# All PSUM banks as one ring in program order, the first layer's weighting in column halves, and a new order of a group's steps

## Chip, cores and metric

One core of one Trainium2 chip. The metric is the device time of one execution in microseconds (us).

## The reference

Four cross-attention layers run one after another on x (64 batches x 64 tokens x 256 features), each against the same context ctx (64 x 64 x 256). Inputs are float32, the mask is all ones in the drawn inputs, and the weights of all layers are inputs too.

```
L0 (channels = the 64 tokens): Mn = Wn inorm(x) + bn;  Mm = Wm inorm(ctx) + bm;  A = softmax(Mn' Mm) over 256
                               x = Wo (Ml A') + bo + x,  Ml = Wl ctx + bl
L1, L2 (16 heads of 16):       a = layer_norm(ctx) * gamma + beta;  Q = x Wq', K = a Wk', V = a Wv'
                               x = x + tanh(gate) * (softmax(mask(Q K' / 4)) V) Wo'
L3 (one head):                 q = x w_q', k = ctx w_k', v = ctx w_v'
                               x = x + alpha * (softmax(q k' / 16) v) w_o'
```

## The kernel before

The 64 batches are cut into 8 groups of 8 (`GB`), four pairs of batches (`NP`) of 128 tokens each. A prologue prepares the weights and the first group's "front" (transposes of x and ctx, their normalised forms, Mn, Mm, V0). Then a loop runs seven times over one group, with the front of the next group worked in, and an eighth, last group follows without a front.

What stands in a group is a list of steps made by `group_order` (from line 37 on). Every engine walks the same list and does its own part of each step. A step (kind, layer, i) is one of:

- P name i, a projection or transpose by TensorE into one PSUM bank: K, V, Q (keys, values, queries of a layer), AT (transposed attention output), O (output projection), XN, PV (last layer's output), and in the front xT, cT, nT, Mn, Mm, V0. An E step of the same name says where ScalarE and VectorE take the result out of the bank, where that isn't the place of the P step itself.
- S l i, scores. Layers 0 to 2 have eight, which TensorE makes in pairs (i even makes i and i + 1, each in 64 rows of the array, line 565 or 582). VectorE takes the maximum (lines 916, 920) and, in layers 1 and 2, subtracts it (line 924), which releases the bank. In layer 0 the exp on ScalarE reads the bank and releases it.
- X l i, the exp on ScalarE (lines 749, 755).
- T l i, transposes of the exps by TensorE (lines 608, 615), copied from PSUM by ScalarE (line 767). In layers 1 and 2 a T step fills two banks.
- A l i, the weighting of the values by TensorE (line 635 in layer 0, line 652 in layers 1 and 2), then division by the sums on VectorE. In layer 0 two A steps share a bank; in layers 1 and 2 the two batches of a pair go to partitions 0 to 63 and 64 to 127, in 64-column halves of the array.
- ST, MV, SC: statistics and moments of the next group's rows, and the sum columns, on VectorE.

Projections of layers 1 to 3 are made of a high and a low part of each operand, three products (lines 361 to 363). The low part of attnT is `o - hi` on VectorE (line 888), of the state it is line 857, and O waits for the first, Q for the second. Queries go from PSUM to `qe` in two copies on ScalarE (line 732), value rows in four (line 719), keys in one (line 712), whose rows GpSimd spreads into `kbd` (line 1119).

The eight PSUM banks are four rings of two: `proj`, `scores`, `turned`, `weighted`. The dictionary `RING` puts xT, cT, nT and V0 into the `weighted` ring. Before a fill TensorE waits until the fill two before in the same ring is released; `*_full` and `*_free` semaphores of each bank count fills and releases. In the prologue all eight banks serve as one ring.

The layer 0 weighting, from line 633:

```
for u in range(2):
    for s in range(2):
        mm_ = pe.matmul(o[:, (2 * (i % 2) + u) * V0W:(2 * (i % 2) + u + 1) * V0W],
                        probsT[:, i % 4, D * s + P * u:D * s + P * u + P], v0[:, i, s, :], start=s == 0, stop=s == 1)
```

SyncE loads the next group (`load_group`, lines 318 to 321) once the proj banks' fills of the group before are counted and `normed` and `mix_ready` are reached, and stores the result in two parts (line 334). It waits for the landed store at the end of a pass, so the next pass's load is issued behind it. GpSimd makes `mix`, the reciprocal deviations and the normalised rows (`front`, lines 1140 to 1161), between spreading the keys of layer 1 and of layer 2. The first scores of layer 2 wait for that second spreading.

Of the kernel before, what the change touches and what calls it, by code (L numbers as in the profile page):

```python
# [17 lines left out]
ALU = mybir.AluOpType  # L18
# [18 lines left out]
def group_order(front):  # L37
# [17 lines left out]
    def S(l, i):  # L55
        return at("S", l, i)
# [64 lines left out]
RING = {"xT": "A", "cT": "A", "nT": "A", "V0": "A"}  # L121


def build(nc, x, ctx_in, mask, w, cst, out):
# [8 lines left out]
    def numbered(order, kind):  # L133
        n, at = 0, {}
        for s in order:
            if kind == "A" and s[0] == "A" and s[1] == 0:
                at[s] = n
                n += s[2] % 2
            elif (RING.get(s[1], "P") if s[0] == "P" else s[0]) == kind:
                per = 2 if kind == "T" and s[1] in (1, 2) else 1  # L140
                at[s] = n
                n += per
        return at, n

    p_at, p_n = numbered(ORDER, "P")
    p_at_last, _ = numbered(LAST_ORDER, "P")
    pro_steps = [s for s in PROLOGUE if s[0] == "P"]
    p_at_pro, p_n_pro = {s: n for n, s in enumerate(pro_steps)}, len(pro_steps)
    s_at, s_n = numbered(ORDER, "S")
    t_at, t_n = numbered(ORDER, "T")  # L150
    a_at, a_n = numbered(ORDER, "A")
    assert p_n % 2 == 0 and s_n % 2 == 0 and t_n % 2 == 0 and a_n % 2 == 0

    pro_bank = {s: (n + 2 - p_n_pro) % 8 for s, n in p_at_pro.items()}
    PRO_FILLS = [list(pro_bank.values()).count(i) for i in range(8)]
    P_BASE = PRO_FILLS[0]
    assert P_BASE == PRO_FILLS[1] > 1

    def p_count(g, step, last):

        if g is None:
            bank_of = pro_bank[step]
            return bank_of, sum(pro_bank[s] == bank_of and n <= p_at_pro[step] for s, n in p_at_pro.items())
        n = (p_at_last if last else p_at)[step]
        return n % 2, g * (p_n // 2) + (P_BASE + n // 2 + 1)

    def ring_count(g, n, total):


        fills = g * (total // 2) + (n // 2 + 1)  # L170
        return n % 2, fills, g * (total // 2) + (n // 2 + 2)

    with ExitStack() as stack:
# [75 lines left out]
        negmax = sb("negmax", [P, 2, NJ])  # L249
        shifted = sb("shifted", [P, 2, 512])  # L250
# [16 lines left out]
        bl_wide, bo_row = result[:, 0, 0:P], result[:, 1, 0:C]  # L267

        scores = [bank("scores0"), bank("scores1")]
        turned = [bank("turned0"), bank("turned1")]  # L270
        weighted = [bank("weighted0"), bank("weighted1")]
        proj = [bank("proj0"), bank("proj1")] + scores + turned + weighted

# [37 lines left out]
        def _(sp):  # L311
# [11 lines left out]
            def iteration(g, last):  # L323
                if not last:

                    for i in range(2):
                        hold(proj_full[i], g * (p_n // 2) + P_BASE)
# [909 lines left out]
```

## Time and profile before

| | us |
|---|---|
| median of 3 runs | 837.75 (830.71 to 838.94) |
| profiled execution: its time | 832.73 |
| profiled execution: its span, first to last instruction | 830.9 |
| mean granted TensorE clock of that execution | 0.978 |
| matmuls | 7362 |

The profile is of one execution. A row's time is from the start of its instruction to its end; the ends of matmuls are modelled, so that the distance from one step's first row to the next step's is a better measure of a step than its busy time. PE is TensorE's matmuls and PEld its weight loads. A fp32 matmul stands as two instructions, each with its load. "idle before <-X" means that the engine stood before the instruction and X let it go.

### The profile page before, as it was taken

The numbers are of one execution on the slowest core, as the hardware profiler recorded it, in microseconds if no ns is written. First come the engines' busy times: TensorE is split into PE (matmuls) and PEld (weight loads), VectorE is DVE, ScalarE is ACT, GpSimd is POOL, SyncE is SP. The second block draws the span as 40 slices with busy tenths as digits, with TensorE's granted clock in tenths as the row PEclk, the third lists the DMA queues.
The fourth block names the chain that finished last, engine by engine and source line by source line (L and its number), as shares of the span: only waits on it lengthen the run. The fifth ranks groups of instructions, "written<-read, shape, count | busy, mean of one in ns | idle before, by whom it ended". The sixth has DMA issues, their size and how long they took to land.

```text
span 830.9 us, 19359 instructions
## 1 busy us (share of the span) xinstructions
PE 719.0 (87%) x7362; PEld 645.1 (78%) x7362; DVE 526.5 (63%) x1148; ACT 459.1 (55%) x909; POOL 199.8 (24%) x169
## 2 busy tenths in 40 slices
PE   2689889988998889998899889998899888988886
PEld 2578788877888788887788778887888877878775
DVE  4957567675676656674675746756566745745565
ACT  1486555655547555565556555475554655546452
POOL 3543400442004700136004420047001360010000
PEclk9899999999999999999999999999999999999999
DMA  7010000200001000200002000010002000000000
GB/s 207 27 55 1 2 2 0 79 0 0 0 26 53 0 0 0 79 0 0 0 0 79 0 0 0 25 54 0 0 0 79 0 0 0 0 27 2 1 2 26
DMA packets 18805, 17.14 MB, mean 21 GB/s; under 512 B 2206, under 2 KB 18718, under 8 KB 18782
## 3 DMA queue, kind: packets, MB, share of 16 engines
q1 hardware_dynamic: 16854, 15.38, 5.7%
q10 hardware_dynamic: 1608, 1.18, 0.5%
q0 software_dynamic: 320, 0.27, 0.2%
q8 instruction: 15, 0.25, 0.1%
q14 instruction: 8, 0.07, 0.0%
HBM read 12.63 MB, written 4.19 MB: 20 GB/s over the span
## 4 chain that ended last, share of the span: by engine, by line
PE 52%; DVE 22%; ACT 14%; issue 10%; DMA 1%; DVEq 1%; ACTq 0%; POOL 0%
PE proj L361 8%; PE scores L582 8%; DVE negmax L920 8%; PE proj L362 7%; PE proj L363 7%; DVE shifted L924 5%; ACT work L732 4%; PE weighted L635 3%; PE scores L565 3%; PE turned L615 3%; ACT v L719 3%; PE turned L608 3%; DVE attnT_lo L888 2%; PE weighted L652 2%; ACT work L749 2%
## 5 line engine op out<-in xcount | busy, mean ns | idle before, releaser
L767 ACT ACTIVATE work<-turned 128x512 f32<-128x512 f32 (+1 forms) x208 | 114.0, 580 | 106.2 <-PE turned L615 70.7
L1119 POOL TENSOR_TENSOR kbd<-k_tmp,own_row 128x1024 f32<-128x1024 f32 x32 | 60.3, 1894 | 444.5 <-ACT k_tmp L712 444.5
L755 ACT ACTIVATE work<-shifted 128x512 f32<-128x512 f32 x128 | 80.6, 631 | 86.4 <-DVE shifted L924 86.3
L920 DVE TENSOR_REDUCE negmax<-scores 128x8 f32<-128x512 f32 x128 | 87.4, 683 | 45.2 <-PE scores L582 45.2
L582 PE MATMUL scores<-kbd,work 64*128 64x128 f32 x1024 | 75.3, 286 | 42.0 <-DVE shifted L924 29.4
L582 PEld LDWEIGHTS scores<-kbd,work 64*128 64x128 f32 x1024 | 63.8, 189 | 48.9 <-issue 35.2
L924 DVE TENSOR_TENSOR shifted<-scores,negmax 128x512 f32<-128x512 f32 x128 | 88.5, 691 | 5.4
L916 DVE TENSOR_REDUCE negmax<-scores 128x2 f32<-128x512 f32 x64 | 41.2, 686 | 66.5 <-PE scores L565 66.3
L652 PEld LDWEIGHTS weighted<-v,work 128*64 128x64 f32 x2048 | 65.5, 138 | 21.9 <-issue 19.7
L652 PE MATMUL weighted<-v,work 128*64 128x34 f32 x2048 | 72.1, 225 | 8.3 <-ACT work L767 8.3
L615 PE MATMUL turned<-const,work 128*128 128x128 f32 x512 | 70.0, 281 | 1.7 <-ACT work L755 1.2
L984 DVE RECIPROCAL recip<-weighted 128x16 f32<-128x16 f32 x64 | 16.1, 251 | 85.8 <-PE weighted L652 85.8
L749 ACT ACTIVATE work<-scores,negmax 128x256 f32<-128x256 f32 x128 | 52.9, 478 | 29.2 <-DVE negmax L916 29.0
L635 PE MATMUL weighted<-v,work 128*128 128x65 f32 x512 | 66.0, 272 | 2.4 <-issue 2.4
L635 PEld LDWEIGHTS weighted<-v,work 128*128 128x128 f32 x512 | 62.1, 192 | 5.5 <-issue 4.3
L719 ACT ACTIVATE v<-proj,mask_col 64x256 f32<-64x256 f32 x128 | 61.2, 478 | 8.5 <-PE proj L363 7.3
L615 PEld LDWEIGHTS turned<-const,work 128*128 128x128 f32 x512 | 57.3, 143 | 6.4 <-ACT work L755 1.3
L361 PE MATMUL proj<-attnT_hi,wT_o_hi 128*128 128x256 f32 x128 | 39.9, 312 | 22.6 <-DVE attnT_lo L888 22.4
L361 PEld LDWEIGHTS proj<-attnT_hi,wT_o_hi 128*128 128x128 f32 x128 | 24.6, 192 | 28.3 <-DVE attnT_lo L888 28.3
L732 ACT ACTIVATE work<-proj,const 128x512 f32<-128x512 f32 x64 | 40.5, 686 | 7.5 <-PE proj L363 7.0
L888 DVE TENSOR_TENSOR attnT_lo<-proj,attnT_hi 128x512 fp32r<-128x512 f32 x32 | 22.0, 689 | 31.5 <-ACT attnT_hi L737 31.5
L897 DVE SCALAR_TENSOR_TENSOR state<-proj,o_bias,state 128x256 f32<-128x256 f32 x64 | 28.0, 478 | 19.0 <-PE proj L363 19.0
(210 smaller groups left out, 1782.6 us busy)
## 6 DMA issues: line engine op xcount, KB each, us to landing
x_raw<-in_x_dram SPq DMA_DIRECT2D x8, 512.0 KB, 4.8
c_raw<-in_ctx_dram SPq DMA_DIRECT2D x8, 512.0 KB, 6.4
out_dram<-attn SPq DMA_DIRECT2D x16, 256.0 KB, 2.1
mrow_u<-in_mask_dram SPq DMA_DIRECT2D x8, 64.0 KB, 3.9
scratch<-in_L_xattn_ln_beta_dram POOLq DMA_DIRECT2D x2, 128.0 KB, 5.6
work<-in_L_xattn_Wq_dram ACTq DMA_DIRECT2D x1, 256.0 KB, 7.9
work<-in_L_xattn_Wk_dram ACTq DMA_DIRECT2D x1, 256.0 KB, 4.5
work<-in_L_xattn_Wv_dram ACTq DMA_DIRECT2D x1, 256.0 KB, 4.1
```

The source lines that it names most:

```text
L361: pe.matmul(o, lh, rh, start=first, stop=False)
L582: mm_ = pe.matmul(dst, qe[rows, c, i + h].rearrange("p q t -> p (q t)"), kbd[l - 1][rows, c, i + h], start=True, stop=True)
L615: mm_ = pe.transpose(o[:, P * j:P * j + P], e[:, 4 * c + j, :], ident)
L635: mm_ = pe.matmul(o[:, (2 * (i % 2) + u) * V0W:(2 * (i % 2) + u + 1) * V0W], probsT[:, i % 4, D * s + P * u:D * s + P * u + P], v0[:, i, s ...
L652: mm_ = pe.matmul(o[C * q:C * q + C, 2 * VW * (4 * c + j):2 * VW * (4 * c + j + 1)], e[:, j, q, :], v2[l - 1][:, i, 2 * (4 * c + j) + q].r ...
L719: ins = act.activation(v2[int(name[1]) - 1][rows, 2 * i + q, :, h, 0:HD], o[rows, D * q:D * q + D].rearrange("k (n v) -> k n v", n=NH), AC ...
L732: ins = act.activation(qe[:, :, 4 * i:4 * i + 4, q, :], o[:].rearrange("p (k b t) -> p k b t", k=NK, t=C), ACT.Identity, scale=parity[:, q ...
L749: ins = act.activation(probs[:, i % 4, D * u:D * u + D], scores[bk][:, D * u:D * u + D], ACT.Exp, bias=negmax[:, i % 2, u:u + 1])
L755: act.activation(e, shifted[:, i % 2, :].rearrange("t (c k) -> t c k", c=NK), ACT.Exp).then_inc(exps, 1)
L767: act.activation(probsT[:, slot, 0:width], turned[bk][:, 0:width], ACT.Copy).then_inc(turned_free[bk], 1)
L920: dve.tensor_reduce(negmax[:, i % 2, :], sv, AX_X, ALU.max, negate=True).then_inc(rowmax, 1)
L924: dve.tensor_tensor(shifted[:, i % 2, :].rearrange("t (j k) -> t j k", k=C), sv, negmax[:, i % 2, :].unsqueeze(2).broadcast_to([P, NJ, C]) ...
```

## The change

Four things are done together.

1. The four rings become one, `psum`: `fills_of` numbers all fills of a group in program order (104 of them, 13 to a bank), and fill n takes bank n mod 8. The semaphores are `full` and `freed`, one pair a bank, and `wait_banks` merges all waits of a step on one bank into one. SyncE counts eight `full` semaphores instead of two.
2. A(0,i) does each 128-column product as two of 64 columns, for the two halves of the output partitions.
3. `negmax0` has its own column for each score step of layer 0, instead of two used in turn.
4. `group_order` lists all steps anew, and gives many of them an E step of their own. The last group's list is the same one without the front steps.

```diff
-    o += S(0, 0) + S(0, 1) + X(0, 0) + X(0, 1) + p("K1", 0) + p("K1", 1)
-    o += S(0, 2) + S(0, 3) + copied("K1", 0) + T(0, 0) + X(0, 2) + T(0, 1) + X(0, 3) + copied("K1", 1) + A(0, 0) + p("V1", 0)
-    o += S(0, 4) + S(0, 5) + T(0, 2) + A(0, 1) + X(0, 4) + T(0, 3) + X(0, 5) + copied("V1", 0) + A(0, 2) + p("V1", 1)
-    o += S(0, 6) + S(0, 7) + T(0, 4) + A(0, 3) + X(0, 6) + T(0, 5) + X(0, 7) + copied("V1", 1) + A(0, 4) + nxt(("ST", 0)) + nxt(("ST", 1))
-    o += T(0, 6) + A(0, 5) + p("Q1", 0) + T(0, 7) + A(0, 6) + nxt(("ST", 2)) + S(1, 0) + S(1, 1) + X(1, 0) + X(1, 1) + A(0, 7)
-    o += nxt(("ST", 3)) + nxt(("MV", 0))
-    o += S(1, 2) + S(1, 3) + p("K2", 0) + X(1, 2) + X(1, 3) + p("Q1", 1) + T(1, 0) + copied("Q1", 1) + p("K2", 1)
-    o += A(1, 0) + S(1, 4) + S(1, 5) + T(1, 1) + X(1, 4) + X(1, 5)
-    o += A(1, 1) + S(1, 6) + S(1, 7) + T(1, 2) + X(1, 6) + X(1, 7) + p("K3", 1) + p("AT1", 0)
-    o += A(1, 2) + p("O1", 0) + T(1, 3) + p("K3", 0) + p("V2", 0) + p("Q2", 0)
-    o += A(1, 3) + S(2, 0) + S(2, 1) + X(2, 0) + X(2, 1) + p("AT1", 1) + p("V2", 1)
-    o += S(2, 2) + S(2, 3) + X(2, 2) + X(2, 3) + p("O1", 1) + T(2, 0) + p("V3", 0) + (p("V3", 1) if front else []) + p("Q2", 1)
...
+    o += S(0, 0) + S(0, 1) + p("V1", 0) + X(0, 0) + X(0, 1) + p("K1", 0) + copied("V1", 0) + T(0, 0) + S(0, 2) + S(0, 3)
+    o += p("K1", 1) + X(0, 2) + T(0, 1) + X(0, 3) + copied("K1", 1) + S(0, 4) + S(0, 5) + X(0, 4) + A(0, 0) + X(0, 5)
+    o += A(0, 1) + T(0, 2) + T(0, 3) + nxt(("ST", 0)) + S(0, 6) + S(0, 7) + X(0, 6) + p("V1", 1) + A(0, 2) + nxt(("ST", 1))
+    o += A(0, 3) + T(0, 4) + T(0, 5) + T(0, 6) + A(0, 4) + X(0, 7) + A(0, 5) + p("Q1", 0) + A(0, 6) + T(0, 7)
+    o += nxt(("ST", 2)) + S(1, 0) + S(1, 1) + A(0, 7) + p("K2", 0) + X(1, 0) + S(1, 2) + S(1, 3) + X(1, 1) + nxt(("ST", 3))
+    o += p("K2", 1) + T(1, 0) + p("Q1", 1) + nxt(("MV", 0)) + X(1, 2) + copied("Q1", 1) + A(1, 0) + X(1, 3) + S(1, 4)
+    o += S(1, 5) + T(1, 1) + X(1, 4) + S(1, 6) + S(1, 7) + X(1, 5) + A(1, 1) + p("K3", 1) + T(1, 2) + X(1, 6)
+    o += copied("K3", 1) + X(1, 7) + p("AT1", 0) + A(1, 2) + T(1, 3) + p("O1", 0) + copied("O1", 0) + A(1, 3) + p("K3", 0)
+    o += p("Q2", 0) + p("AT1", 1) + p("V2", 0) + S(2, 0) + S(2, 1) + X(2, 0) + p("O1", 1) + f("Mn", 0) + X(2, 1) + p("V3", 0)
+    o += S(2, 2) + S(2, 3) + p("V2", 1) + T(2, 0) + p("Q2", 1) + X(2, 2) + p("V3", 1) + A(2, 0) + copied("Q2", 1) + S(2, 4)
+    o += S(2, 5) + X(2, 3) + T(2, 1) + copied("V3", 1) + A(2, 1) + S(2, 6) + S(2, 7) + X(2, 4) + X(2, 5) + f("cT", 0)
+    o += p("AT2", 0) + T(2, 2) + nxt(("E", "cT", 0)) + X(2, 6) + X(2, 7) + f("xT", 0) + f("Mn", 1) + f("xT", 1) + A(2, 2)
+    o += T(2, 3) + nxt(("E", "xT", 1)) + p("O2", 0) + A(2, 3) + S(3, 0) + p("AT2", 1) + X(3, 0) + f("cT", 1) + p("XN", 0)
+    o += f("Mm", 0) + nxt(("E", "cT", 1)) + copied("XN", 0) + p("O2", 1) + nxt(("E", "Mm", 0)) + f("nT", 0) + f("Mm", 1)
+    o += T(3, 0) + S(3, 1) + p("XN", 1) + f("nT", 1) + X(3, 1) + nxt(("E", "nT", 1)) + p("PV", 0) + f("V0", 0) + T(3, 1)
+    o += f("V0", 1) + p("PV", 1) + nxt(("E", "V0", 0))
+    return o
...
+    def fills_of(order):
+        fills = []
+        for step in order:
+            kind, l, i = (step + (0,))[:3]
+            if kind == "P" or kind == "S" or kind == "A" and (l or i % 2 == 0):
+                fills.append(step + (0,))
+            elif kind == "T":
+                fills += [step + (c,) for c in range(2 if l in (1, 2) else 1)]
+        banks = {f: n % 8 for n, f in enumerate(fills)}
...
                     for u in range(2):
+                        cols = slice((2 * (i % 2) + u) * V0W, (2 * (i % 2) + u + 1) * V0W)
                         for s in range(2):
-                            mm_ = pe.matmul(o[:, (2 * (i % 2) + u) * V0W:(2 * (i % 2) + u + 1) * V0W],
-                                            probsT[:, i % 4, D * s + P * u:D * s + P * u + P], v0[:, i, s, :],
-                                            start=s == 0, stop=s == 1)
+                            for q in range(2):
+                                t0 = D * s + P * u + C * q
+                                mm_ = pe.matmul(o[C * q:C * q + C, cols], probsT[:, i % 4, t0:t0 + C], v0[:, i, s, :],
+                                                start=s == 0, stop=s == 1)
...
-                dve.tensor_reduce(negmax[:, i % 2, 0:2], s[:].rearrange("t (u k) -> t u k", u=2), AX_X, ALU.max,
+                dve.tensor_reduce(negmax0[:, i, :], s[:].rearrange("t (u k) -> t u k", u=2), AX_X, ALU.max,
```

## Rows read from the trace of the kernel before

**Rows 1.** The page's first part: busy time and share of the span by engine.

```profile
PE 719.0 (87%) x7362; PEld 645.1 (78%) x7362; DVE 526.5 (63%) x1148; ACT 459.1 (55%) x909; POOL 199.8 (24%) x169
```

**Rows 2.** Timeline of SyncE's queue: start, length, line, operation; stores and loads.

```profile
339.93 2.61 SPq L334 DMA_DIRECT2D out_dram<-attn  x2
345.14 0.37 SPq L318 DMA_DIRECT2D mrow_u<-in_mask_dram  x1
...
437.15 2.61 SPq L334 DMA_DIRECT2D out_dram<-attn  x2
...
534.27 2.61 SPq L334 DMA_DIRECT2D out_dram<-attn  x2
```

**Rows 3.** Windows: stretch, length, busy PE, PEld, DVE, ACT, POOL; clock, DMA.

```profile
341.10:363.20 22.10, 21.50 (x187) 19.36 (x186) 13.17 (x31) 16.03 (x36) 9.15 (x7) 1.00 0.22 70
363.20:395.50 32.30, 27.41 (x308) 24.14 (x308) 19.14 (x44) 16.52 (x30) 15.27 (x12) 0.95 0.00 0
395.50:438.30 42.80, 38.98 (x420) 35.37 (x420) 30.24 (x64) 22.70 (x43) 0.00 (x0) 1.00 0.00 2
...
437.30:534.40 97.10, 86.46 (x915) 77.71 (x914) 62.41 (x139) 55.34 (x108) 24.43 (x19) 1.00 0.05 17
...
sum 99.40, PE 83.57 PEld 73.97 DVE 53.63 ACT 50.32 POOL 7.58; mean PE 27.86 PEld 24.66 DVE 17.88 ACT 16.77 POOL 2.52
```

**Rows 4.** PE's waits from 340.0 to 437.2: who for whom, us, times, longest.

```profile
PE scores L582 <- DVE shifted L924: 3.6, 4, 1.9
PE proj L361 <- DVE attnT_lo L888: 2.9, 3, 1.3
```

**Rows 5.** Timeline of PE and POOL: start, length, line, out<-in, count, idle before.

```profile
351.40 1.00 PE L635 MATMUL weighted<-v,work 128*128 128x65 f32 x8
352.24 0.60 PE L608 MATMUL turned<-const,work 128*128 128x128 f32 x4
352.83 0.62 POOL L1140 TENSOR_SCALAR c_norm<-mrow_u 128x512 f32<-128x512 uint8 x1 [0.93 <-DMA c_raw<-in_ctx_dram]
...
367.26 1.36 PE L582 MATMUL scores<-kbd,work 64*128 64x128 f32 x16 [1.88 <-DVE shifted L924]
...
374.63 0.40 PE L362 MATMUL proj<-nT_lo,wT_k_hi 128*128 128x512 f32 x1
374.86 0.40 PE L363 MATMUL proj<-nT_hi,wT_k_lo 128*128 128x512 f32 x1
375.19 1.13 PE L652 MATMUL weighted<-v,work 128*64 128x34 f32 x32
376.25 1.16 PE L582 MATMUL scores<-kbd,work 64*128 64x128 f32 x16
...
378.77 1.13 PE L652 MATMUL weighted<-v,work 128*64 128x34 f32 x32 [0.34 <-ACT work L767]
...
382.79 3.75 POOL L1119 TENSOR_TENSOR kbd<-k_tmp,own_row 128x1024 f32<-128x1024 f32 x2
```

**Rows 6.** Groups by line and form, 340.0 to 437.2: busy, mean ns, idle before.

```profile
L635 PEld LDWEIGHTS weighted<-v,work 128*128 128x128 f32 x64 | 7.8, 192 | 0.6 <-issue 0.5
L652 PEld LDWEIGHTS weighted<-v,work 128*64 128x64 f32 x256 | 8.2, 138 | 2.4 <-issue 2.1
...
L924 DVE TENSOR_TENSOR shifted<-scores,negmax 128x512 f32<-128x512 f32 x16 | 11.1, 691 | 0.6
L920 DVE TENSOR_REDUCE negmax<-scores 128x8 f32<-128x512 f32 x16 | 10.9, 682 | 5.1 <-PE scores L582 5.1
```

**Rows 7.** Timeline of ScalarE in part A of the same group.

```profile
347.31 0.83 ACT L749 ACTIVATE work<-scores,negmax 128x256 f32<-128x256 f32 x2
348.02 0.61 ACT L767 ACTIVATE work<-turned 128x512 f32<-128x512 f32 x1
...
349.21 0.72 ACT L712 ACTIVATE k_tmp<-proj,k_bias 128x512 f32<-128x512 f32 x1
...
359.23 1.95 ACT L719 ACTIVATE v<-proj,mask_col 64x256 f32<-64x256 f32 x4
```

More of the change, by code:

```diff
@@ L145, in build @@
[L145 to L155, printed above, removed]
@@ L156, in build @@
-    P_BASE = PRO_FILLS[0]
-    assert P_BASE == PRO_FILLS[1] > 1
-    def p_count(g, step, last):
-        if g is None:
[L162 to L171, printed above, removed]
+    def fills_of(order):
[7 more added lines that the diff above has]
+        banks = {f: n % 8 for n, f in enumerate(fills)}
+        nth = {f: n // 8 + 1 for n, f in enumerate(fills)}
+        return banks, nth, [list(banks.values()).count(b) for b in range(8)]
@@ L431, in proj_step @@
-                used = [("P", "AT" + name[1], i)] if name in ("O1", "O2") else []
+                used = {"O1": [("P", "AT1", i)], "O2": [("P", "AT2", i)], "PV": [("T", 3, i)]}.get(name, [])
+                if name in ("AT1", "AT2"):
+                    used = [("A", int(name[2]), 2 * i + q) for q in range(2)]
                 if g is None and name in ("Mn", "Mm", "V0"):
                     used = [("P", "W0" if name == "V0" else "W0T", 0)]
-                wait_copied(g, last, used, filling=None if g is not None and name in RING else step)
+                o, signal = start_fill(g, step, last, consumed=used, front=fronts("nT") if name == "K1" and i == 0 else ())
@@ L708, in proj_step @@
                 elif name in ("K1", "K2"):
-                    o, free = full(g, step, last)
+                    o, free = filled(g, step, last)
                     l = int(name[1])
@@ L713, in proj_step @@
                 elif name in ("V1", "V2"):
-                    o, free = full(g, step, last)
+                    o, free = filled(g, step, last)
                     act.sem_inc(act_held, 1)
@@ L735, in proj_step @@
                 elif name in ("AT1", "AT2"):
-                    o, _ = full(g, step, last)
+                    o, _ = filled(g, step, last)
                     act.activation(attnT[0][:].rearrange("f q (b t) -> f q b t", t=C),
@@ L772, in weight_step @@
                     return
-                o, free = full(None, step, False)
+                o, free = filled(None, step, False)
                 v = o[:].rearrange("h (k m) -> h k m", k=NK)
@@ L862, in proj_step @@
                 if name == "V0":
-                    o, free, _ = full(g, step, last)
+                    o, free, _ = filled(g, step, last)
                     for q in range(2):
@@ L870, in proj_step @@
                 elif name in ("cT", "nT"):
-                    o, free, _ = full(g, step, last)
+                    o, free, _ = filled(g, step, last)
                     hi, lo = cT if name == "cT" else nT
@@ L876, in proj_step @@
                 elif name in ("Mn", "Mm"):
-                    o, free, _ = full(g, step, last)
+                    o, free, _ = filled(g, step, last)
                     (hi, lo), col = (mn, 0) if name == "Mn" else (mm, 1)
@@ L885, in proj_step @@
                 elif name in ("AT1", "AT2"):
-                    o, free, _ = full(g, step, last)
+                    o, free, _ = filled(g, step, last)
                     dve.wait_ge(attn_hi, 4 * g + (2 * int(name[2]) - 1 + i))
@@ L892, in proj_step @@
                 elif name in ("O1", "O2"):
-                    o, free, n = full(g, step, last)
+                    o, free, n = filled(g, step, last)
                     l = int(name[1])
@@ L1017, in weight_step @@
                     return
-                o, free, n = full(None, step, False)
+                o, free, n = filled(None, step, False)
                 if name == "W0T":
```

311 lines of the change are left out of this document (127 added, 184 removed).

## Prediction

> **What bounds the kernel now.** I read the page first, then each group's windows, then the waits and the timelines of one group. TensorE (PE) is busy 87% of the span, VectorE 63%, ScalarE 55% [rows 1]. One loop pass takes from one store issue to the next, 437.15 - 339.93 = 97.2 us [rows 2]. I count time t in a pass from its first score matmul, at 341.1, and cut the pass in three: A, first layer, to S(1,0) at t = 22.1; B, second layer, to S(2,0) at t = 54.4; C, third and fourth layer and next group's front, to 97.2. PE idles 22.1 - 21.5 = 0.6 us in A, 32.3 - 27.4 = 4.9 in B, 42.8 - 39.0 = 3.8 in C [rows 3]. ScalarE, in A, is busy 16.0 of 22.1. So no engine is full: the pass is set by PE's program order, whose in-order matmuls stand behind chains over VectorE and ScalarE. The waits show which: a score bank that VectorE has not released (3.6 us a pass) and the low part of the attention transpose (2.9) [rows 4]. The longest, 1.88 us at 367.26, is of S(1,2) for a bank of the two-bank score ring that S(1,0) still holds [rows 5], while PE had K2, Q1 and others to do that need no score bank.
>
> The clock is part of it. In B the mean granted clock is 0.95 of the 2.4 GHz level, in the part with the most idle time; A and C have 1.00 [rows 3]. Over 32.3 us that is 1.6 us of work. But the next pass has 1.00 throughout [rows 3] and lasts 534.27 - 437.15 = 97.1 us [rows 2]: other chains cover it, so I count nothing for it.
>
> **The arithmetic that changes.** A(0,i) is 8 weight loads and matmuls of 128 columns by 65; it takes 352.24 - 351.40 = 0.84 us [rows 5], 105 ns a pair. After: 16 of 64 columns by 65. No row has that. The nearest is the later layers' A, 32 of 64 by 34 in 376.25 - 375.19 = 1.06 us, 33 ns each. If weight loads pace it, the 65 cost the same: 16 x 33 = 0.53 us. If moving columns pace it, 65/34 x 33 = 63 ns, 1.01 us. I take 0.53: a load of 128 columns lasts 192 ns and one of 64 lasts 138, 54 ns for 64 columns, 0.84 ns a column, and 128 x 0.84 = 108 is the 105 of the old pair [rows 6], so loads pace it. Kept for the range: 0.53 to 1.01. In and out of the halved form I add 0.1 us each: the first half matmul at 375.19 comes 0.33 behind the start of a matmul whose like follow at 0.23 [rows 5]. Eight more such changes a pass, 0.8 us. The work on PE thus falls by 8 x 0.31 - 0.8 = 1.7 us; at the other end it grows by 8 x 0.17 + 0.8 = 2.2.
>
> The Trainium skill ("TensorE: Matmul & The Clock Gate", Part 3) says that a weight load overlaps matmuls in flight only where the row group differs. Column halves share their rows. By that rule load and matmul would run one behind the other. The rows speak against it: 33 ns between starts, with loads of 138 ns [rows 5, 6].
>
> **The order, walked.** I put the new list of steps beside the rows: a step on PE costs the distance from its first row to the next step's, the evacuations their rows, each engine in its list's order, each bank free when the fill eight before is released.
>
> A. VectorE now takes V0(0) behind the last PV, then the sum columns: S(0,0)'s maximum is out at t = 3.1 (before 2.4). From there ScalarE is full: 8 exp steps at 0.75 (0.71 and more between starts), two K copies at 0.7, two V copies at 1.95, seven turn copies at 0.55 (0.48 to 0.6) [rows 7], in all 15.2, so t = 18.3. A(0,4) waits for the copy of T(0,4) at 16.4, then A(0,4), A(0,5), Q1(0) at 1.42 on PE to 19.0, the query copy 1.27 from 19.2: S(1,0) at 20.5 against 22.1. A(0,7) takes 0.3 less too. Gain 1.6. The halves matter little here, since ScalarE hides them: at 0.84 a step S(1,0) would come 0.5 later and A(0,7) end 0.9 later; at 1.01, 1.6 later.
>
> B. K2(0) fills the hole before S(1,2): its two banks come from T(0,6) and A(0,4), both long free, so the 1.88 us go and S(1,2) starts at 23.8 (before 26.2). K2(1), T(1,0), Q1(1), A(1,0) follow without a gap to 29.9; S(1,4) waits for the query copy (0.5). S(1,6) stands ahead of A(1,1) and uses the time in which A waited 0.34 for its copy [rows 5]. T(1,3) waits 0.6 for the last exp, O1(0) 0.4 for the low part instead of 1.3 (T(1,3) and A(1,2) stand in its shadow). K3(0) covers the state split (1.1 us on VectorE), AT1(1) and V2(0) the query copy: S(2,0) at 48.6, so B is 28.1 long instead of 32.3. Gain 4.2, of 4.9 + 1.6 there at most.
>
> C. O1(1), Mn(0), V3(0) cover S(2,0)'s evacuation; S(2,2) no longer waits 0.9. S(2,4) waits 0.3, A(2,1) 0.5. cT, xT, Mn(1) fill the third layer's tail where O2(0) waited. PE ends at t = 87.3. C is 38.7 instead of 42.8. Gain 4.1. What is late next: T(2,3) behind the exp, T(3,1) behind the last normalisation.
>
> The walk gives 9.9 a pass, 87.3 long. Before's rows hold waits of 0.3 us marked "issue" or behind copies that such a walk leaves out, about three a pass [rows 4, 5]; I take 1.0 off: 8.9.
>
> **Costed at nothing, and what hides it.** Statistics of the next group move on VectorE from t = 18.9 to 11.0, where they wait for all three loads. The loads are issued at 345.14, behind the landed store, at t = 4.0, and POOL's wait for them ends at 352.83, t = 11.7 [rows 2, 4]. SP's loads stay where they were, it only waits on eight banks instead of two, all filled before. So VectorE stands 0.7 us with S(0,6)'s maximum queued behind, and the exp of it is wanted at t = 13.2 against 13.0: hidden with 0.2 to spare. Each microsecond that the loads land later costs up to one in A. The moments come 0.8 us later than before in the walk. POOL's normalisation and second spreading of keys hang on them; the spreading ended at 382.79 + 3.75, t = 45.4 [rows 5], and will at 46.2, and S(2,0), now at 48.6, has 2.4 us left where it had 9. POOL's queue isn't otherwise moved. negmax0 has a slot for each i and removes no instruction. Merged waits on PE are fewer or the same.
>
> **Sum.** Seven passes x 8.9 = 62.3. The last, without the front steps, is 99.4 long and idles 99.4 - 83.6 = 15.8 us of it [rows 3]; it has no front work to fill its tail, the same A and B: 8.9 too. The prologue has the same steps in the same order: 0. The profiled run took 832.7 us; 832.7 - 71.2 = 761.5. The median of the runs is 837.75, 5 above it; I lean half way: 764.
>
> **Rivals.**
> (1) As walked: 764, own range 748 to 782. For: the banks wanted are free in the walk by 0.5 us or more at all but four places. Chance 0.49.
> (2) Half the gain: the waits go from the ring to ScalarE's queue, which takes copies in list order, a V copy of 1.95 us ahead of a turn copy that PE wants. A is already such a stretch. 4.5 us a pass: 832.7 - 36 = 797, with the halves at 1.01 or not. Chance 0.26.
> (3) Loads and matmuls of the halves run serially (the rule cited above): 80 ns a pair (read as serial, the old pair's 105 ns [rows 5] is half load, half matmul; half of the load gone leaves some 80). A(0,i) 1.3 us, S(1,0) 2.0 later, A(0,7) 2.5: 6.4 a pass, 781. Chance 0.04.
> (4) Better than walked, with the slow clock gone and counting: 10.5 a pass, 749 or less. Chance 0.05.
> (5) The change does nothing measurable: VectorE's chain from maximum to release, 1.33 us a score step over 16 steps [rows 6], and the chain from the attention transpose over its copy and low part to O, on which PE waits 2.9 us [rows 4], set the pass in whatever order. Against: VectorE is busy 62.6 of 97.2 us. 825 to 842. Chance 0.08.
> (6) Slower: one ring in program order. Every fill, also of a step that had banks of its own, now waits for the fill eight before, so one late evacuation stops all. There are 104 / 8 = 13 rounds a pass. Tightest are S(0,5) behind the V1(0) copy (0.5 us in the walk), S(2,7) behind V3(1), T(2,3) behind cT(0). If a round loses 0.68 us more than walked the gain is gone; at 1.0, 13 - 8.9 = 4.1 us a pass: 865. Against: before's rings of two were stricter for scores and turns. Chance 0.08.
>
> About 1% is what a measurement of this kernel can tell from no change. Faster: 0.49 + 0.26 + 0.04 + 0.05 = 0.84; same 0.08; slower 0.08. The range of 8 in 10 runs from (4)'s edge through (2): 745 to 810.
>
> **What would show it.** Right: passes of 87 to 89 us between stores; S(1,0) at t = 20.5, S(2,0) at 48 to 49; no wait of scores for VectorE above 0.5 us; halves at 33 ns between starts; clock 1.00 in B. Step A is wrong if halves run at 63 ns or more, or if VectorE waits for a load beyond t = 12. Step B is wrong if S(2,0) comes after 50. The whole is wrong if PE's waits name the copies of V, K or cT as releasers of other steps' banks, (6), or if ScalarE's queue has no idle time in B, (2).

## The result and the profile after

The changed kernel takes 788.1 us (median of 4 runs, 786.1 to 790.3). The kernel before, run beside it, takes 834.2 (830.7 to 838.9). The ratio is 0.944 (95% interval 0.938 to 0.951): faster by 46 us, inside the forecast range, and 24 us above the forecast of 764. The profiled execution took 790.3 us, its span 788.5, its mean granted clock 0.983.

First the page of after, busy time by engine, which answers to [rows 1]:

```profile
PE 700.9 (89%) x7874; PEld 619.9 (79%) x7874; DVE 570.0 (72%) x1148; ACT 455.3 (58%) x909; POOL 200.6 (25%) x169
```

TensorE has 512 matmuls more (the halves) and 18 us less work. VectorE has the same 1148 instructions as before and is 570.0 - 526.5 = 43.5 us longer busy. This is the line that the forecast did not expect. Nothing in the diff makes a VectorE instruction bigger.

The timeline of SyncE's queue of after, stores (start, length, line, operation), answers to [rows 2]:

```profile
140.82 2.13 SPq L309 DMA_DIRECT2D out_dram<-attn  x2
...
326.19 2.14 SPq L309 DMA_DIRECT2D out_dram<-attn  x2
418.19 2.14 SPq L309 DMA_DIRECT2D out_dram<-attn  x2
510.02 2.14 SPq L309 DMA_DIRECT2D out_dram<-attn  x2
604.64 2.15 SPq L309 DMA_DIRECT2D out_dram<-attn  x2
697.70 87.73 SPq L309 DMA_DIRECT2D out_dram<-attn  x4
```

The pass after 326.19 is 92.0 us long, the six between the first and the last row (697.70 - 140.82) / 6 = 92.8 on average, against 97.2 before. The forecast said 88.3. The last group is different: from its neighbour's store (697.70 here, 728.84 before) to the end of the span it takes 90.8 us where before took 102.1, a gain of 11.3 and more than the 8.9 forecast. So what was lost is lost in the passes that have a front, and not in the last one.

Who waits for whom on TensorE, whole span of after (us, times, longest), answers to [rows 4]:

```profile
PE psum L336 <- DVE state_lo L799: 24.7, 15, 2.6
...
PE psum L588 <- ACT work L712: 10.5, 8, 1.4
PE psum L533 <- issue: 7.6, 23, 0.4
```

No score step waits for VectorE's release any more. The first line is new (before had 0.3 us of it): the queries (L336) wait 24.7 us for the low part of the state, 15 times, in seven passes 3.5 each. The groups by line and form of after say why (busy us, mean ns of one, idle before):

```profile
L797 DVE CAST state_hi<-state 128x512 fp32r<-128x512 f32 x32 | 41.8, 1307 | 1.1
...
L910 DVE TENSOR_TENSOR state<-k3T,xT 128x256 f32<-128x256 f32 x32 | 35.0, 1095 | 1.1
L588 PEld LDWEIGHTS psum<-v,work 128*64 128x64 f32 x1024 | 34.0, 138 | 17.7 <-ACT work L712 11.3 <-issue 1.2
```

The same two groups of the kernel before:

```profile
L972 DVE TENSOR_TENSOR state<-k3T,xT 128x256 f32<-128x256 f32 x32 | 17.3, 540 | 1.1
L855 DVE CAST state_hi<-state 128x512 fp32r<-128x512 f32 x32 | 13.7, 427 | 1.1
```

The cast that makes the state's high part grew from 427 to 1307 ns, the sum that adds the first layer's result to the state from 540 to 1095. Together that is 28.1 + 17.7 = 45.8 us, all of the 43.5 and a little more. Neither is shown as idle time: both stand as busy. The timeline of VectorE, GpSimd (POOL) and the queries of after, in one pass (start, length, line, out<-in, count, idle before), shows where; the pass began at 326.95:

```profile
337.32 1.90 POOL L1056 TENSOR_TENSOR kbd<-k_tmp,own_row 128x1024 f32<-128x1024 f32 x1 [3.23 <-ACT k_tmp L658]
337.39 2.10 DVE L910 TENSOR_TENSOR state<-k3T,xT 128x256 f32<-128x256 f32 x1
...
341.41 1.04 POOL L1085 TENSOR_TENSOR c_norm<-c_norm,mix_col 128x512 f32<-128x512 f32 x1 [0.25 <-POOL mix L1078]
341.60 0.41 DVE L931 BATCH_NORM_STATS2 stats<-c_raw 128x6 f32<-128x256 f32 x1
...
342.53 1.26 POOL L1088 TENSOR_TENSOR c_norm<-c_norm,const 128x512 f32<-128x512 f32 x1
342.58 1.49 DVE L910 TENSOR_TENSOR state<-k3T,xT 128x256 f32<-128x256 f32 x1
343.87 1.34 POOL L1091 TENSOR_TENSOR mix<-c_norm,mix 128x512 f32<-128x512 f32 x1
344.11 1.39 DVE L797 CAST state_hi<-state 128x512 fp32r<-128x512 f32 x1
...
346.28 0.39 PE L336 MATMUL psum<-state_hi,wT_q_hi 128*128 128x256 f32 x1 [0.97 <-DVE state_lo L799]
...
346.81 0.43 DVE L910 TENSOR_TENSOR state<-k3T,xT 128x256 f32<-128x256 f32 x1
...
366.95 4.84 POOL L1098 TENSOR_SCALAR x_norm<-x_raw,mean_var,rstd 128x256 f32<-128x256 f32 x4
...
371.76 3.75 POOL L1056 TENSOR_TENSOR kbd<-k_tmp,own_row 128x1024 f32<-128x1024 f32 x2
372.30 3.49 DVE L797 CAST state_hi<-state 128x512 fp32r<-128x512 f32 x1
...
376.57 0.39 PE L336 MATMUL psum<-state_hi,wT_q_hi 128*128 128x256 f32 x1 [2.57 <-DVE state_lo L799]
...
380.05 1.16 PE L533 MATMUL psum<-kbd,work 64*128 64x128 f32 x16
```

The sum takes 2.10 us where it starts under a GpSimd instruction and 0.43 where none runs. The statistics at 341.60, which read one SBUF tensor, take their 0.41 under a GpSimd instruction as elsewhere. The cast behind O1(0) starts at 372.30, half a microsecond into GpSimd's second key spreading, and ends at 375.79, when that has ended (371.76 + 3.75 = 375.51). Q2(0) waits 2.57 us for it, and S(2,0) comes at t = 53.1 instead of 48.6. In the kernel before the spreading ended at t = 45.4 [rows 5], and this cast came at t = 48.2: they missed each other by 2.8 us. The new order brings it forward to t = 45.4, while GpSimd's chain hangs on the loads and the moments and ends at t = 48.6. The moments are there at t = 32.1 (359.06 - 326.95), before at 29.0 (370.12 - 341.1): 3.1 us later in the pass, where the forecast had 0.8.

### The profile page after: what moved, and what is told of

Read it like the earlier page. It is cut to its first block, busy times and chain, and to the rows that moved or that the text cites. A ratio compares the mean times of both kernels' runs of the same rounds, so it can differ in the third digit from the quotient of the medians.

```text
span 788.5 us, 20133 instructions
## 1 busy us (share of the span) xinstructions
PE 700.9 (89%) x7874; PEld 619.9 (79%) x7874; DVE 570.0 (72%) x1148; ACT 455.3 (58%) x909; POOL 200.6 (25%) x169
## 4 chain that ended last, share of the span: by engine, by line
PE 69%; DVE 15%; issue 6%; ACT 5%; SPq 2%; DMA 2%; DVEq 0%; ACTq 0%
PE psum L336 10%; PE psum L533 9%; PE psum L338 8%; PE psum L337 8%; PE psum L601 7%; PE psum L561 6%; DVE state_hi L797 4%; PE psum L416 3%; PE psum L588 2%; PE psum L520 2%; PE psum L411 2%; PE psum L543 2%; DVE state L910 2%; DVE negmax L856 2%; ACT work L712 2%
## 5 line engine op out<-in xcount | busy, mean ns | idle before, releaser
L712 ACT ACTIVATE work<-psum 128x512 f32<-128x512 f32 (+1 forms) x208 | 111.7, 585 | 52.6 <-PE psum L561 39.3
L860 DVE TENSOR_REDUCE negmax<-psum 128x8 f32<-128x512 f32 x128 | 87.6, 684 | 39.3 <-PE psum L533 38.3
L864 DVE TENSOR_TENSOR shifted<-psum,negmax 128x512 f32<-128x512 f32 x128 | 88.5, 692 | 5.4
L533 PE MATMUL psum<-kbd,work 64*128 64x128 f32 x1024 | 74.4, 284 | 7.7 <-issue 7.6
L533 PEld LDWEIGHTS psum<-kbd,work 64*128 64x128 f32 x1024 | 62.6, 187 | 17.8 <-issue 15.4
L601 PEld LDWEIGHTS psum<-v,work 128*64 128x64 f32 x2048 | 65.1, 138 | 12.8 <-issue 7.5
L601 PE MATMUL psum<-v,work 128*64 128x34 f32 x2048 | 72.1, 225 | 3.1 <-ACT work L712 3.1
L665 ACT ACTIVATE v<-psum,mask_col 64x256 f32<-64x256 f32 x128 | 61.5, 480 | 23.0 <-PE psum L338 21.8
L561 PE MATMUL psum<-const,work 128*128 128x128 f32 x512 | 68.1, 276 | 1.4 <-ACT work L701 0.6
L678 ACT ACTIVATE work<-psum,const 128x512 f32<-128x512 f32 x64 | 40.4, 681 | 45.8 <-PE psum L338 45.5
L336 PE MATMUL psum<-state_hi,wT_q_hi 128*128 128x256 f32 x128 | 40.7, 318 | 24.7 <-DVE state_lo L799 24.7
L561 PEld LDWEIGHTS psum<-const,work 128*128 128x128 f32 x512 | 56.8, 141 | 6.8 <-ACT work L701 1.6
L830 DVE TENSOR_TENSOR attnT_lo<-psum,attnT_hi 128x512 fp32r<-128x512 f32 x32 | 22.0, 689 | 46.5 <-ACT attnT_hi L683 46.2
L336 PEld LDWEIGHTS psum<-state_hi,wT_q_hi 128*128 128x128 f32 x128 | 25.8, 201 | 29.1 <-DVE state_lo L799 28.0
L588 PEld LDWEIGHTS psum<-v,work 128*64 128x64 f32 x1024 | 34.0, 138 | 17.7 <-ACT work L712 11.3
L797 DVE CAST state_hi<-state 128x512 fp32r<-128x512 f32 x32 | 41.8, 1307 | 1.1
L336 PE MATMUL psum<-attnT_hi,wT_o_hi 128*128 128x256 f32 x128 | 39.0, 305 | 3.4 <-DVE attnT_lo L830 3.3
```

What stands on the lines that cost most here:

```text
L336: pe.matmul(o, lh, rh, start=first, stop=False)
L533: mm_ = pe.matmul(dst, qe[rows, c, i + h].rearrange("p q t -> p (q t)"), kbd[l - 1][rows, c, i + h], start=True, stop=True)
L561: mm_ = pe.transpose(o[:, P * j:P * j + P], e[:, 4 * c + j, :], ident)
L588: mm_ = pe.matmul(o[C * q:C * q + C, cols], probsT[:, i % 4, t0:t0 + C], v0[:, i, s, :], start=s == 0, stop=s == 1)
L601: mm_ = pe.matmul(o[C * q:C * q + C, 2 * VW * (4 * c + j):2 * VW * (4 * c + j + 1)], e[:, j, q, :], v2[l - 1][:, i, 2 * (4 * c + j) + q].r ...
L712: act.activation(probsT[:, slot, 0:width], o[:, 0:width], ACT.Copy).then_inc(free, 1)
```

## The experiments

The theory, P: after the reordering, VectorE's casts and sums between SBUF tensors stand while GpSimd's instructions run, and this costs what is missing to the forecast. Rivals: Q, the loss is ScalarE's queue and the ring (rivals 2 and 6 of the forecast); O, only part of the change counts (the halves or the ring alone). All ratios are to the kernel before, run beside each.

### GpSimd's work taken away, in both kernels

Both kernels below leave work out: they spread one of eight batches' keys, build a quarter of `mix` and normalise 16 of 256 columns.

```diff
-                    each = [P, GB, 2, C]
-                    pool.tensor_tensor(kbd[l - 1][:, i], k_tmp[:, i, :].rearrange("p (b s) -> p b s", s=C).unsqueeze(2).broadcast_to(each),
+                    each = [P, 1, 2, C]
+                    pool.tensor_tensor(kbd[l - 1][:, i, 0:1], k_tmp[:, i, :].rearrange("p (b s) -> p b s", s=C)[:, 0:1].unsqueeze(2).broadcast_to(each),
...
-                    ins = pool.tensor_scalar(dst[:, t % NP, :], src[:, t % NP, :], mean_var[:, t, 0:1], rstd[:, t:t + 1],
+                    ins = pool.tensor_scalar(dst[:, t % NP, 0:16], src[:, t % NP, 0:16], mean_var[:, t, 0:1], rstd[:, t:t + 1],
```

In the kernel after:

> The changed kernel with GpSimd's work in the loop cut to an eighth or less (keys of one batch of eight spread, the rest stays zero; a quarter of mix; 16 of 256 columns normalised), so that part of the computation is left out; number and order of all steps, waits and the other engines' work are unchanged. Theory P: all long forms vanish, the state sum of the first layer back to 0.43 and the high-part copy to 0.43; passes of 87 to 88 us as in the walk, total 750 to 760. Theory S or R: passes stay at 92, total 780 to 788.

Measured 752.8 us (751.9 to 754.5), ratio 0.905 (0.901 to 0.908). Groups by line of this kernel:

```profile
L910 DVE TENSOR_TENSOR state<-k3T,xT 128x256 f32<-128x256 f32 x32 | 15.0, 467 | 1.1
L797 DVE CAST state_hi<-state 128x512 fp32r<-128x512 f32 x32 | 13.7, 427 | 1.1
```

Both groups are back, the wait on the state's low part is gone from TensorE's list, and the six passes between stores average 88.0 us. The walk had given 88.3.

The control, in the kernel before:

> The kernel before with GpSimd's work cut in the same way as in the changed one (that part of the computation is left out). Theory P: in the kernel before only the first layer's state sums meet GpSimd (mean 540 ns against 424 for the like form), no high-part copy does (427 ns in all 32); so at most 0.5 us a pass, 830 to 834. If less work on GpSimd helped in some general way, as fewer rows to wait for, it would come down here by 30 us too.

Measured 834.2 us, ratio 1.001 (0.998 to 1.004). The cast is 427 ns as ever, the sum falls from 540 to 431. So GpSimd's work costs the old order nothing and the new order 35 us. P stands, and Q cannot explain this pair: ScalarE's queue and the ring are the same in after and in its small-GpSimd form. As the kernel without this work also has earlier keys and normalised rows, it is an upper bound on what the collisions cost. The next experiments keep all work.

### The key spreading moved ahead

```diff
+                spread_keys(g, 2, False)
                 deviations(nth)
...
                 front(g)
-                spread_keys(g, 2, False)
```

With it Mn(0) on TensorE waits for the normalised rows.

> The changed kernel with one move on GpSimd: layer 2's keys are spread before the next group's deviations and normalised rows, not behind them (and Mn(0) waits for the normalised rows by itself). Theory P (VectorE's copies from SBUF to SBUF stand still while a GpSimd instruction runs): the high-part copy behind O1(0), 3.49 us in every pass, falls to 0.43, Q2(0) on TensorE no longer waits 2.6 us, seven times: about 18 us less than the changed kernel's 788, 770. The collisions in the first layer stay. Theory S (ScalarE's queue in list order sets the pass): the spreading is off the path, 788 within 3. Theory R (the ring of eight banks sets it): 788 within 3 too.

Measured 776.0 us (774.6 to 777.8), ratio 0.933 (0.929 to 0.937). Timeline of this kernel, VectorE and GpSimd:

```profile
346.50 1.90 POOL L1058 TENSOR_TENSOR kbd<-k_tmp,own_row 128x1024 f32<-128x1024 f32 x1 [8.44 <-ACT k_tmp L660]
346.83 1.84 DVE L912 TENSOR_TENSOR state<-k3T,xT 128x256 f32<-128x256 f32 x1
...
366.15 0.43 DVE L799 CAST state_hi<-state 128x512 fp32r<-128x512 f32 x1
```

The cast behind O1(0) is back at 0.43, and TensorE's wait on the low part falls from 24.7 to 11.0 us. P had said 770. The 6 us between: the moved spreading now falls on the last sum of the first layer (1.84 us at 346.83), a place where after had none. Q1(1) on TensorE now waits 0.66 us a pass for the low part behind it (349.92), 4.6 of the 6. Moving a GpSimd instruction moved the collision.

### The sum in a form that reads one operand from PSUM

After multiplies the weighted values by the reciprocals into SBUF and adds two SBUF operands. This kernel does both in one instruction, four of 64 columns a step, whose only large SBUF input is `xT`:

```diff
-                    dve.tensor_tensor(x_scaled, sums[:, :, :, 0:C], rz.unsqueeze(3).broadcast_to([P, 2, 2, C]),
-                                      ALU.mult).then_inc(free, 1)
...
+                            ins = dve.scalar_tensor_tensor(out=state[:, u, toks], in0=sums[:, h, u, 0:C], scalar=rz[:, h, u:u + 1],
+                                                           in1=xT[:, u, toks], op0=ALU.mult, op1=ALU.add)
```

> The changed kernel with the first layer's division and addition of xT on VectorE in one kind of instruction: four scalar_tensor_tensor of 64 columns that read the sums in PSUM and xT in SBUF, in place of a product into SBUF and a sum of two SBUF tensors. Theory P, with the port as the thing that both want: an instruction with one SBUF input doesn't stand still behind GpSimd, so none of the four is stretched, where the old sum was 2.1 and 1.4 us in A(0,1) and A(0,3). The copy behind it (1.39) stays stretched. 1 to 1.5 us a pass of part A: 788 - 10 = 778. If any VectorE instruction stands still while GpSimd runs, nothing is won: 788 to 792 (four instructions are a little longer than two).

Measured 784.6 us (783.1 to 785.9), ratio 0.941 (0.938 to 0.944). Timeline of this kernel:

```profile
335.91 0.86 DVE L909 SCALAR_TENSOR_TENSOR state<-psum,recip,xT 128x64 f32<-128x64 f32 x4
336.29 1.89 POOL L1056 TENSOR_TENSOR kbd<-k_tmp,own_row 128x1024 f32<-128x1024 f32 x1 [3.21 <-ACT k_tmp L658]
...
341.64 1.17 DVE L797 CAST state_hi<-state 128x512 fp32r<-128x512 f32 x1
...
342.85 1.66 DVE L799 TENSOR_TENSOR state_lo<-state,state_hi 128x512 fp32r<-128x512 f32 x1
```

All 128 such instructions take 277 ns on average, under the spreading as elsewhere: none stands. So it is not GpSimd's running as such that stops VectorE, but which operands VectorE's instruction has. The expected 778 was missed by 7 us: TensorE's wait on the low part stays at 24.8 us. The cast right behind still stands (1.17 at 341.64), the low part behind it, 0.69 in after, now stands too (1.66), and so does the cast behind O1(0).

### All of it together

The two edits above, and GpSimd starts on `mix` only when the first cast is done:

```diff
+                if g is not None:
+                    hold(state_hi, 4 * g + 1)
```

> Fused sums, layer 2's keys spread first, and GpSimd's mix held until the first high-part copy of the pass is done: all of GpSimd's work is there, but no VectorE instruction that needs the port meets it. Theory P: passes of 88 us and 752 to 762, as with small GpSimd work (753). Theory S: 776 as with the keys first alone.

Measured 757.3 us (755.0 to 759.7), ratio 0.910 (0.906 to 0.913), as expected. All work is done. This is 31 us faster than the changed kernel. Stores of this kernel:

```profile
311.08 2.15 SPq L309 DMA_DIRECT2D out_dram<-attn  x2
399.67 2.15 SPq L309 DMA_DIRECT2D out_dram<-attn  x2
488.38 2.15 SPq L309 DMA_DIRECT2D out_dram<-attn  x2
```

and its waits on TensorE:

```profile
PE psum L590 <- ACT work L714: 6.5, 8, 1.5
...
PE psum L336 <- DVE state_lo L801: 1.7, 8, 0.3
```

Passes are 88.6 and 88.7 us (88.2 on average over six), and S(2,0) stands at t = 49.75 (361.54 - 311.79) where the walk had 48.6. One collision a pass is left, a cast of 1.40 at 338.21 under the spreading, which costs TensorE almost nothing (0.3 us a pass at most).

### The statistics behind the maxima

What is left over the walk lies in part A, where S(1,0) comes at t = 21.5 and not at 20.5. The timeline of VectorE and ScalarE in the kernel of the last section:

```profile
324.24 0.43 DVE L933 BATCH_NORM_STATS2 stats<-x_raw 128x6 f32<-128x256 f32 x1 [1.58 <-DMA c_raw<-in_ctx_dram]
...
324.91 1.27 DVE L858 TENSOR_REDUCE negmax<-psum 128x2 f32<-128x512 f32 x2
325.62 0.84 ACT L697 ACTIVATE work<-psum,negmax 128x256 f32<-128x256 f32 x2 [1.08 <-DVE negmax L858]
```

VectorE stands 1.58 us for the next group's context rows, up to t = 12.45, with the maxima of S(0,6) queued behind, and the exp stands for them. The loads are issued at t = 5.0 in after (331.99 on SyncE's queue), 1.0 later than before, where the forecast had left them at 4.0. In after itself the rows show no such wait: the sum that stands until 339.49 covers the same time, so that the first collision of the pass costs nothing. The edit puts the first step of the statistics behind the maxima:

```diff
-    o += A(0, 1) + T(0, 2) + T(0, 3) + nxt(("ST", 0)) + S(0, 6) + S(0, 7) + X(0, 6) + p("V1", 1) + A(0, 2) + nxt(("ST", 1))
+    o += A(0, 1) + T(0, 2) + T(0, 3) + S(0, 6) + S(0, 7) + nxt(("ST", 0)) + X(0, 6) + p("V1", 1) + A(0, 2) + nxt(("ST", 1))
```

> The kernel with all three remedies (757.3 us), and in it one step moved: the first statistics of the next group stand on VectorE behind the maxima of S(0,6) and S(0,7) and not ahead of them. In that kernel VectorE waits 1.58 us at t = 12.45 for the loaded context rows with these maxima queued behind, the exp of S(0,6) waits 1.08 us, and A(0,4) 1.34 us for its turn copy. Theory L (in part A what is left over the walk is the wait for the loads, which the forecast costed at nothing): the exp starts 1.08 us earlier, A(0,4) at t = 16.1 instead of 17.2, S(1,0) at 20.5 instead of 21.5; VectorE's wait on the load is below 0.5 us; 757.3 - 7 x 1.0 = 750 us. Rival S (ScalarE is full in part A whatever VectorE does, or later chains take the microsecond back): A(0,4) still waits over 1 us, or S(2,0) stays at t = 49.8; 756 to 758 us.

> The kernel with all three remedies once more, as the yardstick of the run beside it: 757 us, between 755 and 760, by every theory.

Measured 752.6 us (751.6 to 756.6), ratio 0.904 (0.901 to 0.907), beside 758.4 (755.5 to 760.5) for the same kernel without the edit. The gain is 5.8 us, 0.8 a pass. Theory L holds: timeline of this kernel's TensorE,

```profile
327.37 1.18 PE L590 MATMUL psum<-v,work 128*64 128x65 f32 x32 [0.29 <-ACT work L714]
...
331.68 1.16 PE L535 MATMUL psum<-kbd,work 64*128 64x128 f32 x16 [0.30 <-issue]
...
359.98 1.16 PE L535 MATMUL psum<-kbd,work 64*128 64x128 f32 x16
```

where the pass began at 311.28. A(0,4) stands at t = 16.1 (expected 16.1, walked 16.4), S(1,0) at 20.4 (walked 20.5) and S(2,0) at 48.7 (walked 48.6). VectorE's wait for the rows is gone. The total is 2.6 us above the 750 expected, 1.1 of it because the same kernel without the edit ran at 758.4 and not at 757.3. This is the fastest full kernel here, 35 us faster than the changed kernel.

### The halves

With 128 columns at a time again (the loop over `q` taken out), first in after:

> The changed kernel with the first layer's weighting in full columns again, ring and order as changed. By the walk the halves are worth 0.9 us a pass, the rest hidden behind ScalarE: 788 + 7 = 795. If TensorE sets part A: 0.3 us a step, 8 steps, 8 groups: 788 + 19 = 807. If ScalarE or VectorE hide all: 788.

Measured 791.2 us, ratio 0.950 (0.947 to 0.954), 3 us above after; the intervals touch. Then the halves alone, in the kernel before:

> The kernel before with only the column halves. In its part A TensorE idles 0.6 us of 22.1, so if TensorE's order sets it, 0.2 to 0.3 us a step: 834 - 13 = 821. If the chains of ScalarE and VectorE set it (16.0 of 22.1 busy on ScalarE), 830 to 834.

Measured 832.8 us, ratio 0.999 (0.996 to 1.002): nothing. It isn't a clean zero: two casts now fall under GpSimd's instructions (1.38 us instead of 0.43), and TensorE waits 6.0 us for the low part where before waits 0.3. And full columns in the fastest kernel, with a second run of after beside it:

> The kernel whose GpSimd work meets no VectorE copy (757), with the first layer's weighting in full columns. With VectorE's delays gone from the first layer, TensorE and ScalarE alone decide there, as in the walk, which gives the halves 0.9 us a pass: 757 + 7 = 764. If the full difference of the steps on TensorE shows (1.7 us a pass): 771. If ScalarE hides it all: 757.

Measured 767.3 us (765.9 to 769.9), ratio 0.922 (0.918 to 0.926), against 757.3 with halves: 10 us. In the profiled executions a pass is 89.1 us against 88.2, 0.9 longer; the last group is 3.2 longer (92.9 against 89.8), the stretch to the first store 2.4.

> The changed kernel itself, unchanged, beside the kernel before on the same chip as the others: 788 within 3.

Measured 788.3 us, ratio 0.946 (0.942 to 0.949), so after is where it was. The same 0.3 us a step is worth 0, 3 and 10 us in three kernels. In after with full columns a pass at full clock is 91.8 us, with halves 91.8 to 92.0: nothing, and the 3 us come from the last group (95.5 against 90.8) and the start. With full columns TensorE waits 16.9 us for the low part where after waits 24.7: what the halves save in a pass, TensorE waits off again.

### The ring with the old order

After with the steps in the order of before:

> The changed kernel with the step order of the kernel before: the ring of eight banks, the halves and the own columns of negmax0 alone. The wait of S(1,2) for a score bank (1.9 us a pass) and those of S(2,2), S(1,6), S(2,6) (0.4 to 0.9) can go, since the ring frees what two banks held: if the order was bound by rings of two, 2 to 4 us a pass, 834 - 24 = 810. If the order itself carries the gain (theory O), the ring alone gives under 1 us a pass: 826 to 834.

Measured 839.7 us (837.1 to 847.8), ratio 1.007 (1.004 to 1.010): no gain, and by 0.7% slower, with the halves and `negmax0` in it. Collisions with GpSimd don't hide a gain here: the cast has 427 ns in all 32, the sum 487 on average. TensorE's waits in this kernel (its profiled execution is the slowest of the six, 847.8 us at a clock of 0.968):

```profile
PE psum L341 <- DVE attnT_lo L835: 32.2, 25, 1.9
PE psum L341 <- DVE state_lo L804: 16.5, 11, 3.4
...
PE psum L525 <- ACT v L670: 8.8, 8, 1.1
```

The last line is rival (6) in small: scores of the first layer wait 1.1 us a pass for a bank that the copy of V1 (1.95 us, [rows 7]) releases late, only because that bank is now next in turn. In after no step waits for that copy. The wait for the state's low part, 16.5 us, is there without a stretched cast; why is not shown. The opposite experiment, the new order on the four rings of before, was not run, so the ring's share can't be given as a time of its own, and that the order needs the ring is argued and not shown. What is shown is that ring, halves and `negmax0` bring nothing without the new order.

## Why the prediction was right, and why by 24 us too low

The direction came as forecast and 788 lies in the stated range, but outside that of the main case, 748 to 782. The stated range holds it only because it reaches over rival (2), whose 4.5 us a pass is almost the measured 4.4, while its mechanism is not the cause: that is luck. What was right by its own steps:

- **Pass set by TensorE's order, holes filled.** 97.2 us went to 87.6 (store to store, 310.52 to 398.12) in the kernel with the remedies and the statistics moved, S(2,0) at the walk's own time. In after S(1,2) starts without a wait (at t = 25.8, 3.3 behind S(1,0), as walked), and the 3.6 us of waits for the score banks [rows 4] are gone.
- **Halved A(0,i), 33 ns a pair.** After's TensorE, an A(0,i) pair of steps and what follows:

```profile
340.14 1.15 PE L588 MATMUL psum<-v,work 128*64 128x65 f32 x32
341.23 1.53 PE L554 MATMUL psum<-const,work 128*128 128x128 f32 x12
```

  32 products in 341.23 - 340.14 = 1.09 us, 34 ns each, with loads of 138 ns: the weight loads pace them, and the end at 63 ns falls. Rival (3), loads and matmuls one behind the other, would have shown 80. The row group is the same for both halves, so here the measurement stands against the rule of the Trainium skill that the prediction cited ("TensorE: Matmul & The Clock Gate", Part 3). The same part also allows a load into a background weight buffer; whether these loads went that way no run here shows.
- **Part C.** It takes 38.9 us (380.05 to the next pass's first score at 418.94) against 38.7 walked.
- **The worth of the halves**, 0.9 us a pass by the end of A(0,7): 0.9 in the kernel without most collisions. But nothing in a pass of after, and nothing in before. The last group, which the forecast gave the same 0.9, gains 3.2 by them.

Wrong: the step "Costed at nothing, and what hides it", in both its halves. The larger one is GpSimd. The step asked of GpSimd only who waits for its results (S(2,0), with 2.4 us left), and it costed every VectorE instruction at the length it had in the old order. A moved instruction's length depends on what GpSimd runs at that moment. The forecast has both things that meet, the state split under K3(0) and the spreading, whose end it moved from t = 45.4 to 46.2, and did not lay the two engines' rows over one another. An estimate from the rows: in the walk the cast, at 45.4 in after, comes 2.0 us earlier with part A, at 43.4, under a spreading of 3.75 us that ends at 46.2. So the collision was in the forecast's own times. The spreading then ended at 48.6, with the moments 3.1 us late instead of 0.8, and S(2,0)'s 2.4 us were gone as well. Where the cost lies:

- Part B took 30.6 us instead of 28.1: the difference is Q2(0)'s 2.57, waiting for the standing cast.
- Part A took 22.5 instead of 20.5, half of it by the second sum and the cast, which stand one behind the other from 342.58 to 345.50; Q1(0) waits 0.97 us for the low part.
- The other half of A is the second part of the same step, the statistics and their loads. I gave VectorE a stand of 0.7 us, "hidden with 0.2 to spare", with the loads at the t they had before. They come about 1 us later in the pass (GpSimd's wait for them ends at t = 12.6, before at 11.7 [rows 5]), the maxima of S(0,6) with them, ScalarE has no slack in A to take it up, and A(0,4) waits 1.37 us for its turn copy. The forecast had named its price itself, up to one microsecond for each. Rival (2)'s full ScalarE is how the delay is carried, not its cause: without the stand, the same queue gives the walk's time.
- The clock is a third term that the forecast put at nothing. In before, passes at a granted clock of 0.98 take 97.1 to 97.2 us and those at 1.00 take 97.1 to 97.5, so it costs nothing there. In after it does. Windows of two passes (stretch, length, busy PE, PEld, DVE, ACT, POOL; clock, DMA):

```profile
419.90:511.70 91.80, 84.87 (x978) 75.06 (x978) 68.44 (x139) 54.87 (x108) 24.41 (x19) 1.00 0.06 19
511.70:606.30 94.60, 87.61 (x977) 77.63 (x978) 68.47 (x139) 54.87 (x108) 24.41 (x19) 0.96 0.06 19
```

  Three of the six passes between stores have 1.00 and take 92.0 on average, the other three, at 0.96 to 0.98, 93.7: 5.2 us together. In the kernels with three remedies and with the statistics moved all six have 1.00.

The sum of the profiled executions, before to after, in us: up to the first store 145.5 to 140.8, gain 4.7 (forecast 8.9); six passes 6 x (97.2 - 92.8) = 26.5 (forecast 53.4); last group 102.1 to 90.8, 11.3 (forecast 8.9). Together 42.4 against 71.2, so 28.8 are missing. For the six passes the terms close, as an estimate: 3.5 a pass of waits on the low part, 0.8 for the loads (the gain of moving the statistics), 0.9 for the clock, 5.2 together, which is 92.8 less the 87.6 of the kernel without all three. The forecast's 88.3 is 0.7 above that, which leaves 4.5 a pass, 27 in six. The first stretch lacks 4.2, and the last group's extra 2.4 goes the other way.

In the kernel with all three remedies the same sum is 11.0 + 53.9 + 12.3 = 77.2 (its stores at 134.5 and 664.0, the last group 89.8), with the loads' stand still in it. So the walk was too cautious rather than too bold: of the 1.0 us a pass that I took off, 87.6 measured against 87.3 walked leaves 0.3, and the last group, which has no front to collide with, gained more than forecast. Without that caution the forecast would have missed by more.

Of the signs named beforehand, those of "right" fail in after (passes of 92.8 and not 87 to 89, S(1,0) at t = 22.5, S(2,0) at 53.1) and hold in the kernel with the statistics moved. "S(2,0) after 50" came true and pointed at the right part. The words for rival (6), releasers named V, K or cT, did not.

## What to carry to other kernels

When an order of steps is changed, put VectorE's and GpSimd's rows of the planned order side by side, and mark each VectorE instruction that casts within SBUF or has two SBUF inputs: where GpSimd runs, count it to GpSimd's end. After a change compare the mean length of each group with before's; an instruction that stands for another engine looks busy, and no list of waits names it. Reorder such a pair first by putting GpSimd's long instructions where VectorE reads PSUM, and look again afterwards, since the instruction behind can be the next to stand. A saving on TensorE is to be measured again once the waits are gone.

## What the runs showed of the hardware

- VectorE's instruction stands until GpSimd's is through, and over the boundary of two that follow without a gap: the cast that started 0.54 us into two spreadings of 1.9 us each took 3.49 instead of 0.43 us, and ended 0.28 behind the second. With 0.08 us between two GpSimd instructions it got in between them: the sum at 342.58 ended at 344.07, 0.28 behind the first (342.53 + 1.26), though the second had started at 343.87.
- What stood: casts of 128x512 from SBUF to SBUF (0.43 to 3.49 us) and sums of two SBUF operands (0.43 to 2.10). What did not: the sum with one operand in PSUM, under a spreading (277 ns each), and statistics of one SBUF tensor (0.41 at 341.60). The trace agrees with the Trainium skill, "SBUF — State Buffer", section "Who interferes with whom": VectorE's second pair of SBUF ports is GpSimd's too, an exclusive lock for a whole instruction, wanted by casts in the two-port mode and by two SBUF inputs, and not by an instruction with one SBUF input outside that mode. Which mode the cast ran in no run here shows.
- Column halves over the same rows overlap their weight loads: 34 ns a pair with loads of 138 ns, for 65 moving columns as for 34.
- In the other direction GpSimd stands. In the kernel with the spreading moved ahead, VectorE's low part (two SBUF inputs) starts first, and the spreading, 0.10 us later, takes 2.35 us instead of 1.90:

```profile
349.17 0.69 DVE L801 TENSOR_TENSOR state_lo<-state,state_hi 128x512 fp32r<-128x512 f32 x1
349.27 2.35 POOL L1058 TENSOR_TENSOR kbd<-k_tmp,own_row 128x1024 f32<-128x1024 f32 x1 [0.87 <-ACT k_tmp L660]
```
